# A graph network on one core: the gathers of z rows written out on GpSimd, with indices from the loaded table

## The chip, the cores and the metric

The kernel runs on one core of a Trainium2 chip. The metric is the time on the device in microseconds (us), the median of the runs. The engines are TensorE (PE in the profile; PEld its weight loads), VectorE (DVE), ScalarE (ACT), GpSimd (POOL) and SyncE (SP, which here only issues DMAs).

## The reference

A graph of 6250 nodes with 128 features and 200,000 edges, sorted by destination, goes through four graph layers. After each, the layer's result is added to x and normalized:

```python
x = layernorm(x + L0(x, W, attn_w, rel_emb, bias, src, dst, edge_type))   # attention over edges
x = layernorm(x + L1(x, ...))                                            # mean over neighbours
x = layernorm(x + L2(x, ..., edge_weight))                               # three weighted convolutions
x = layernorm(x + L3(x, ..., edge_attr))                                 # filtered messages

# L0
z = h @ W.T
e = leaky_relu((z @ w1)[src] + (z @ w2)[dst])
num = exp(e - segment_max(e, dst)[dst])
alpha = num / segment_sum(num, dst)[dst]
h_agg = segment_sum((rel_emb[etype] * alpha)[:, None] * z[src], dst)
```

## The kernel before

The edges are padded to 196 groups (NG) of 1024, each held as 128 partitions by 8 columns (TILES). The stages are blocks of code, and at the end of a block all engines meet at a barrier.

- A prelude loads inputs and computes z for all nodes. The rows of z, 132 words with the attention scores beside the features (ZW), are stored to HBM as z_table.
- A short block (lines 574 to 722) finds, for each window of 8 destination nodes, which tiles of 128 edges belong to it. GpSimd meanwhile runs gather_pairs(e, 0, 4), the first 8 groups of z rows.
- The main build block (lines 746 to 994) turns the edges into two dense matrices in HBM, c_dense (counts) and w_dense (edge weights), by source block and destination. VectorE makes one-hot tiles in a ring of eight slots (lines 836, 839, 850), with other work on the edge tables between them. TensorE multiplies them into four PSUM windows (line 920). ScalarE copies a finished window to a staging buffer (line 984, into parts of A and H by turns) and clears it (line 968). SyncE stores each full half block of 64 nodes (line 754). A loop at the end repairs windows that a tile overran. GpSimd runs gather_pairs(e, 4, 98), the other 188 groups, on its own.
- The attention layer reads those rows group by group (line 1055). It uses no tile of the build block besides z_edges in HBM and a few tables.
- Then come the dense layers (line 1405), during which GpSimd scatters edge records by an unrolled loop (line 1546), and the last layer, with an unrolled loop of gathers (line 1637).

gather_pairs copies rows of z for every edge of a group into the buffer z_got and stores them to z_edges in HBM. z_got has two slots, used by turns. One gather is one indirect DMA of 128 rows, each chosen by an index in its partition (line 527). Eight make a group, and the group is stored by one DMA (put_group, line 512). Per slot, s_zgot counts landed gathers and s_zput landed stores. The store of a group is issued after the fourth gather of the next one. The order on GpSimd is that of the code. The loop runs over pairs of groups; since its index is a register, the eight index columns of a group are first copied from src_i to z_idx (line 523), and the gathers wait for the copy (s_zidx). The increments of note["pool"] after a wait count for nobody.

Of the kernel before, what the change touches and what calls it, by code (L numbers as in the profile page):

```python
# [6 lines left out]
P = 128  # L7
# [7 lines left out]
TILES = 8  # L15
GE = TILES * P
NG = -(-N_EDGES // GE)
# [50 lines left out]
i32 = mybir.dt.int32  # L68
# [5 lines left out]
def build_program(nc, T, out):  # L74
    ctx = ExitStack()
    with ctx:
        def sb(name, shape, dt=f32, of=ctx):
            return of.enter_context(nc.sbuf_tensor(name, shape, dt))
# [3 lines left out]
        def sem(name):  # L82
            live.append(nc.alloc_semaphore(name=name))
            return live[-1]
# [10 lines left out]
        def dram(name, shape, dt=f32):  # L95
            return nc.dram_tensor(name, shape, dt, kind="Internal").ap()
# [20 lines left out]
        src_i = sb("src_i", [P, NG * TILES], i32)  # L117
# [34 lines left out]
        note = {n: nc.alloc_semaphore(name="note_" + n) for n in ("dve", "pe", "act", "pool", "sp")}  # L152
        Xv = X[:, :].rearrange("p (b f) -> p b f", f=F)
        z_table = dram("z_table", (NP_, ZW))
        z_edges = dram("z_edges", (NG, P, TILES, ZW))
# [344 lines left out]

        building = ctx.enter_context(ExitStack())
        z_got = sb("z_got", [P, 2, TILES, ZW], of=building)
        z_idx = sb("z_idx", [P, 2, TILES], i32, of=building)
        s_zidx = sem("bd_zidx")
        s_zgot, s_zput = ([sem(f"bd_{n}{s}") for s in range(2)] for n in ("zgot", "zput"))
        EARLY_PAIRS = 4

        def gather_pairs(e, lo, hi):
            def put_group(g, s, landed):
                e.wait_ge(s_zgot[s], landed)  # L510
                e.sem_inc(note["pool"], 1)
                e.dma_start(z_edges[bass.ds(g, 1), :, :, :].rearrange("a p t w -> (a p) t w"), z_got[:, s, :, :]
                            ).then_inc(s_zput[s], 16)

            last = e.alloc_register(f"bd_pool_last{lo}")
            e.reg_mov(last, max(2 * lo - 1, 0))
            with e.Fori(lo, hi) as i:
                for s in range(2):
                    g = i * 2 + s
                    with e.If(i > 0):  # L520
                        e.wait_ge(s_zput[s], i * 16)
                        e.sem_inc(note["pool"], 1)
                    e.tensor_copy(z_idx[:, s, :], src_i[:, bass.ds(g * TILES, TILES)]).then_inc(s_zidx, 1)
                    e.wait_ge(s_zidx, g + 1)
                    e.sem_inc(note["pool"], 1)
                    for t in range(TILES):
                        e.indirect_dma_start(  # L527
                            out=z_got[:, s, t, :], out_offset=None, in_=z_table,
                            in_offset=bass.IndirectOffsetOnAxis(ap=z_idx[:, s, t:t + 1], axis=0),
                        ).then_inc(s_zgot[s], 16)  # L530
                        if t == TILES // 2 - 1 and s:
                            put_group(i * 2, 0, (i + 1) * (16 * TILES))
                        elif t == TILES // 2 - 1:
                            with e.If(i > 0):
                                put_group(e.snap(last, min_val=0, max_val=NG - 1), 1, i * (16 * TILES))
                e.reg_mov(last, i * 2 + 1)
            if hi == NG // 2:
                put_group(NG - 1, 1, NG // 2 * 16 * TILES)
                for s in range(2):
                    e.wait_ge(s_zput[s], 16 * (NG // 2))  # L540

# [32 lines left out]
        with nc.Block() as block:  # L574
# [42 lines left out]
            @block.gpsimd  # L617
            def _(e):
                gather_pairs(e, 0, EARLY_PAIRS)
# [129 lines left out]
        with nc.Block() as block:  # L749
# [45 lines left out]
            @block.gpsimd  # L795
            def _(e):
                gather_pairs(e, EARLY_PAIRS, NG // 2)
# [1020 lines left out]
```

## Time and profile before

| | us |
|---|---|
| median of 3 runs | 10863.49 |
| the runs | 10908.15, 10863.49, 10833.27 |
| span of the profiled execution, first to last instruction | 10911.3 |
| GpSimd busy in it | 5544.8 (51%) |
| gathers of z rows, 1568 | 2098.9 |
| copies of index columns, 196 | 117.1 |
| TensorE's matmuls of the build, 14112 | 2519.8 |

The profiled execution is one of its own. It has no separate time beside its span, which lies 3 us above the slowest of the runs shown. In its timeline the short block with the first gathers runs from about 86 to 193 us and the main build block from there to about 3277 us. In the page's 40 slices one digit stands for 272.8 us, so these two blocks are the first twelve digits.

### The profile page before, as it was taken

How to read it: one execution, taken by the hardware profiler on the slowest of the kernel's cores; microseconds unless marked ns; L12 is line 12 of the kernel's file. 1: busy time of each engine (PE TensorE's matmuls, PEld its weight loads, DVE VectorE, ACT ScalarE, POOL GpSimd, SP SyncE). 2: the span in 40 equal slices, each digit the busy share in tenths (PEclk: the TensorE clock that was granted, in tenths of full speed). 3: DMA queues.
4: the chain of work that ended last, by engine and by line, in shares of the span. 5: the costliest groups of instructions: out<-in, count | busy, mean ns of one | idle time of the engine just before them, and what ended most of it. 6: DMA issues, size and time to landing. Idle time of an engine off the chain costs nothing. (4 is left out here: it accounts for less than half of the span.)

```text
span 10911.3 us, 154123 instructions
## 1 busy us (share of the span) xinstructions
PE 8137.0 (75%) x38400; PEld 4981.9 (46%) x38401; DVE 4162.8 (38%) x9898; ACT 3246.9 (30%) x5364; POOL 5544.8 (51%) x5296
## 2 busy tenths in 40 slices
PE   2988888888776666555688797887886777877776
PEld 1544444444435555555333343333334555555554
DVE  5887777643336666665400000000002222222223
ACT  3012345645556665555100000000002222222222
POOL 5888887777710000000355555555434655665664
PEclk7999999999995665666788898888987777877777
DMA  4234455656644333322566576666762222222222
GB/s 113 72 112 137 161 184 201 234 200 205 215 163 144 123 111 105 98 92 88 180 272 238 232 292 229 264 254 227 283 241 81 62 59 59 66 59 58 63 61 53
DMA packets 563180, 1661.60 MB, mean 152 GB/s; under 512 B 115313, under 2 KB 312029, under 8 KB 519494
## 3 DMA queue, kind: packets, MB, share of 16 engines
q1 hardware_dynamic: 324442, 1129.76, 28.3%
q0 software_dynamic: 206976, 473.99, 14.8%
q10 hardware_dynamic: 31536, 54.94, 1.4%
q8 instruction: 130, 2.13, 0.1%
q14 instruction: 96, 0.79, 0.0%
HBM read 1174.46 MB, written 483.82 MB: 152 GB/s over the span
## 5 line engine op out<-in xcount | busy, mean ns | idle before, releaser
L920 PE MATMUL wide<-ring 128*128 128x392 bf16 x14112 | 2519.8, 340 | 541.5 <-DVE ring L850 253.7
L527 POOL DMA_INDIRECT z_got<-z_table,z_idx x1568 | 2098.9, 1339 | 595.2 <-issue 468.7
L1546 POOL DMA_INDIRECT sorted_recs<-dn_rec_in,type_f x1568 | 1523.6, 972 | 1300.1 <-DMA dn_rec_in<-in_records 835.0
L1637 POOL DMA_INDIRECT l_rows<-h_table,l_recs x1568 | 1582.1, 1009 | 1176.0 <-DMA l_recs<-sorted_recs 725.3
L920 PEld LDWEIGHTS wide<-ring 128*128 128x128 bf16 x14112 | 1410.4, 100 | 1650.7 <-issue 900.1
L1405 PE MATMUL wide<-stream,X 128*128 128x512 f32 (+1 forms) x2548 | 1149.3, 602 | 255.2 <-issue 230.3
L1055 POOL DMA_DIRECT2D rows<-z_edges x196 | 103.5, 528 | 2055.9 <-PE wide L362 1849.1
L373 PE MATMUL wide<-rows,onehot 128*128 128x130 f32 x3904 | 858.1, 407 | 283.1 <-DVE A L390 283.1
L373 PE MATMUL wide<-l_rows,l_onehot 128*128 128x128 f32 x3904 | 669.5, 321 | 503.4 <-issue 326.7
L373 PEld LDWEIGHTS wide<-rows,onehot 128*128 128x128 f32 x3904 | 793.8, 310 | 341.4 <-DVE A L390 341.4
L1405 PEld LDWEIGHTS wide<-stream,X 128*128 128x128 f32 x2548 | 493.9, 201 | 876.7 <-issue 869.0
L373 PEld LDWEIGHTS wide<-l_rows,l_onehot 128*128 128x128 f32 x3904 | 596.4, 230 | 560.6 <-issue 358.6
L1532 DVE TENSOR_TENSOR A<-A,wide 128x512 f32<-128x512 f32 (+1 forms) x13 | 8.5, 657 | 2076.4 <-DMA range_src<-small 1751.3
L839 DVE TENSOR_TENSOR ring<-ring,parts 128x1536 bf16<-128x1536 bf16 (+1 forms) x394 | 692.5, 1758 | 65.9 <-issue 65.9
L1405 PE MATMUL wide<-stream,A 128*128 128x512 f32 (+1 forms) x1274 | 576.9, 603 | 126.9 <-issue 123.7
L1736 DVE TENSOR_TENSOR l_rows<-l_filters,l_rows 128x1024 f32<-128x1024 f32 x196 | 240.6, 1228 | 1107.3 <-ACT l_filters L1714 844.8
L968 ACT COPY wide<-zero_f 128x784 f32<-128x784 f32 x788 | 642.2, 815 | 66.1 <-PEq L574 17.1
L1405 PE MATMUL wide<-stream,H 128*128 128x512 f32 (+1 forms) x1274 | 574.9, 602 | 116.4 <-issue 110.3
L836 DVE TENSOR_TENSOR ring<-iota_h,src_r 128x512 bf16<-128x512 f16 (+1 forms) x394 | 271.6, 689 | 1015.6 <-PE wide L920 703.6
L984 ACT COPY A<-wide 128x784 f32<-128x784 f32 x392 | 318.0, 811 | 968.5 <-PE wide L920 844.9
L850 DVE TENSOR_SCALAR ring<-iota_h,slot_at 128x784 bf16<-128x784 f16 (+1 forms) x1568 | 596.6, 443 | 0.0
L1675 PE MATMUL wide<-w_L_gnn_W,l_hid 128*128 128x128 f32 x3136 | 498.6, 312 | 87.3 <-issue 85.8
(260 smaller groups left out, 8430.1 us busy)
## 6 DMA issues: line engine op xcount, KB each, us to landing
stream<-w_dense SPq DMA_DIRECT2D x252, 1792.0 KB
stream<-c_dense SPq DMA_DIRECT2D x84, 1792.0 KB
z_edges<-z_got POOLq DMA_DIRECT2D x196, 528.0 KB
rows<-z_edges POOLq DMA_DIRECT2D x196, 528.0 KB
dst_bc<-in_dst_row SPq DMA_DIRECT2D x196, 512.0 KB
c_dense<-A SPq DMA_DIRECT2D x49, 1568.0 KB
w_dense<-A SPq DMA_DIRECT2D x49, 1568.0 KB
c_dense<-H SPq DMA_DIRECT2D x49, 1568.0 KB
```

Source lines behind the costliest of these rows:

```text
L373: ins = e.matmul(sums_bank[:, 0:width], lhsT=onehot[:, t, :], rhs=group_rows[:, t, 0:width], start=(t == 0), stop=(t == TILES - 1))
L527: e.indirect_dma_start(out=z_got[:, s, t, :], out_offset=None, in_=z_table, in_offset=bass.IndirectOffsetOnAxis(ap=z_idx[:, s, t:t + 1], a ...
L836: e.tensor_tensor(to[:, :, 0, :], iota_h[:, 0:P].unsqueeze(1).to_broadcast([P, n, P]), src_r[:, bass.ds(t, n)].unsqueeze(2).to_broadcast([ ...
L839: e.tensor_tensor(to[:, :, 1:4, :], to[:, :, 0:1, :].to_broadcast([P, n, 3, P]), parts[:, bass.ds(t, n), :].unsqueeze(3).to_broadcast([P, ...
L850: e.tensor_scalar(ring[:, at:at + spans * WC], iota_h[:, 0:spans * WC], slot_at[:, bass.ds(t + k, 1)], None, ALU.is_equal).then_inc(s_made, 1)
L920: ins = e.matmul(banks[:, bass.ds(to[v], 1), int(m > 0), 0:WC].rearrange("p a x -> p (a x)"), lhsT=slots[:, k, m * P:(m + 1) * P], rhs=slo ...
L968: e.copy(pairs[k].rearrange("p (a x) -> p a x", a=2)[:, :, 0:WC], zero_f[:, 0:1].unsqueeze(2).to_broadcast([P, 2, WC])).then_inc(s_gone, 1)
L984: e.copy(staging[k][:, :, :, WN * n:WN * (n + 1)], window(n % 4))
L1405: ins = e.matmul(agg_bank[i % 2][:, 0:w], lhsT=stationary[p][:, b, :], rhs=stream[:, l % STREAMS, 0:w // HB, k, :], start=(b == 0), stop=( ...
L1546: e.indirect_dma_start(out=sorted_recs, out_offset=bass.IndirectOffsetOnAxis(ap=pos_i[:, g * TILES + t:g * TILES + t + 1], axis=0), in_=re ...
L1637: e.indirect_dma_start(out=rows[:, k, t, :], out_offset=None, in_=h_table, in_offset=bass.IndirectOffsetOnAxis(ap=recs[:, k, t, R_DST:R_DS ...
L1675: ins = e.matmul(filtered[:, t * P:(t + 1) * P], lhsT=hid[:, g % 2, t * P:(t + 1) * P], rhs=W["L3_gnn_W2"][:, :], start=False, stop=(t % 4 ...
```

## The change

gather_pairs is written out for all groups instead of looping over pairs. Each gather takes its index column straight from src_i at a fixed place, so z_idx, its copies and s_zidx are gone. The order of gathers and stores, the two slots and the waits for landed gathers and stores stay. The increments of note["pool"] are left out. Nothing else in the program is changed.

```diff
-        z_idx = sb("z_idx", [P, 2, TILES], i32, of=building)
-        s_zidx = sem("bd_zidx")
...
         def gather_pairs(e, lo, hi):
-            def put_group(g, s, landed):
-                e.wait_ge(s_zgot[s], landed)
-                e.sem_inc(note["pool"], 1)
-                e.dma_start(z_edges[bass.ds(g, 1), :, :, :].rearrange("a p t w -> (a p) t w"), z_got[:, s, :, :]
-                            ).then_inc(s_zput[s], 16)
...
-            with e.Fori(lo, hi) as i:
-                for s in range(2):
-                    g = i * 2 + s
-                    with e.If(i > 0):
-                        e.wait_ge(s_zput[s], i * 16)
-                        e.sem_inc(note["pool"], 1)
-                    e.tensor_copy(z_idx[:, s, :], src_i[:, bass.ds(g * TILES, TILES)]).then_inc(s_zidx, 1)
-                    e.wait_ge(s_zidx, g + 1)
-                    e.sem_inc(note["pool"], 1)
-                    for t in range(TILES):
-                        e.indirect_dma_start(
-                            out=z_got[:, s, t, :], out_offset=None, in_=z_table,
-                            in_offset=bass.IndirectOffsetOnAxis(ap=z_idx[:, s, t:t + 1], axis=0),
-                        ).then_inc(s_zgot[s], 16)
...
+            def put_group(g):
+                e.wait_ge(s_zgot[g % 2], (g // 2 + 1) * (16 * TILES))
+                e.dma_start(z_edges[g, :, :, :], z_got[:, g % 2, :, :]).then_inc(s_zput[g % 2], 16)
+
+            for g in range(2 * lo, 2 * hi):
+                if g >= 2:
+                    e.wait_ge(s_zput[g % 2], 16 * (g // 2))
+                for t in range(TILES):
+                    at = g * TILES + t
+                    e.indirect_dma_start(
+                        out=z_got[:, g % 2, t, :], out_offset=None, in_=z_table,
+                        in_offset=bass.IndirectOffsetOnAxis(ap=src_i[:, at:at + 1], axis=0),
+                    ).then_inc(s_zgot[g % 2], 16)
+                    if t == TILES // 2 - 1 and g:
+                        put_group(g - 1)
             if hi == NG // 2:
-                put_group(NG - 1, 1, NG // 2 * 16 * TILES)
+                put_group(NG - 1)
                 for s in range(2):
                     e.wait_ge(s_zput[s], 16 * (NG // 2))
```

On GpSimd, at the start of the main build block, the body of the loop before reads as follows for the first of its two groups (bd_zput0 is the landed stores of slot 0, bd_zidx the copy, bd_zgot1 the landed gathers of slot 1):

```order
L520 UNCONDITIONAL_BRANCH [waits bd_zput0]
L523 ISA
L523 COPY z_idx<-src_i 128x8
L524 REGISTER_ALU
L527 DMA z_got<-z_table,z_idx 128x132 [waits bd_zidx]
L527 DMA z_got<-z_table,z_idx 128x132 x3
L535 ISA
L512 ISA [waits bd_zgot1]
L512 DMA z_edges<-z_got 128x1056
```

In the changed kernel the same engine has this for a group and the first half of the next, at the same place:

```order
L516 DMA z_got<-z_table,src_i 128x132 [waits bd_zput0]
L516 DMA z_got<-z_table,src_i 128x132 x3
L509 DMA z_edges<-z_got 128x1056 [waits bd_zgot1]
L516 DMA z_got<-z_table,src_i 128x132 x4
L516 DMA z_got<-z_table,src_i 128x132 [waits bd_zput1]
```

The copy, its wait, the branches and the register instructions are gone, and the waits for landed stores and gathers stand on the DMAs themselves. No instruction of another engine changes its place.

## Rows read from the trace of the kernel before

**Rows 1.** The page: span; TensorE and GpSimd over 40 slices, busy tenths.

```profile
span 10911.3 us, 154123 instructions
...
PE   2988888888776666555688797887886777877776
...
POOL 5888887777710000000355555555434655665664
```

**Rows 2.** Timeline at the blocks' ends: start, length, instruction [idle before, releaser].

```profile
193.70 0.46 POOL L523 COPY z_idx<-src_i 128x8 int32 x1 [7.37 <-POOLq L574]
...
3079.85 0.58 POOL L512 DMA_DIRECT2D z_edges<-z_got  x1 [8.37 <-DMA z_got<-z_table,z_idx]
...
3241.33 0.37 SPq L754 DMA_DIRECT2D c_dense<-H  x1
...
3277.68 0.56 POOL L1055 DMA_DIRECT2D rows<-z_edges  x1 [197.26 <-PEq L1165]
```

**Rows 3.** Waits, 700 to 2100: total us, times, longest.

```profile
PE wide L920 <- DVE ring L850: 208.0, 48, 5.8
...
DVE ring L836 <- PE wide L920: 180.9, 85, 7.0
```

**Rows 4.** Windows: busy us (instructions) by engine, TensorE clock, DMA share, GB/s.

```profile
core 0: us, PE busy (x) PEld busy (x) DVE busy (x) ACT busy (x) POOL busy (x), PEclk, DMA share, GB/s
...
2200.00:3080.00 880.00, 702.35 (x3907) 387.63 (x3906) 344.19 (x492) 451.92 (x559) 645.64 (x642) 0.97 0.61 206
2900.00:3080.00 180.00, 136.91 (x760) 75.46 (x761) 67.16 (x96) 97.77 (x122) 125.88 (x129) 0.97 0.65 220
3080.00:3200.00 120.00, 97.47 (x561) 54.41 (x559) 46.35 (x67) 74.35 (x92) 0.42 (x1) 1.00 0.40 146
```

**Rows 5.** Groups of GpSimd's instructions, 194 to 3085.

```profile
L527 POOL DMA_INDIRECT z_got<-z_table,z_idx x1504 | 2032.4, 1351 | 571.6 <-issue 449.9 <-POOL z_idx L523 115.6 <-DMA z_got<-z_table,z_idx 3.4
L523 POOL COPY z_idx<-src_i 128x8 int32 x188 | 115.1, 612 | 45.4 <-DMA z_edges<-z_got 37.0 <-POOLq L574 7.4
```

**Rows 6.** Timeline of GpSimd across one copy.

```profile
3059.60 0.97 POOL L527 DMA_INDIRECT z_got<-z_table,z_idx  x1 [0.80 <-issue]
3060.88 0.94 POOL L527 DMA_INDIRECT z_got<-z_table,z_idx  x1 [0.30 <-issue]
```

**Rows 7.** Lines 523 and 527: duration ns min/median/max.

```profile
L523 POOL COPY z_idx<-src_i x196: 187/218/3392, 86.1 to 3058.6; 128x8 int32 x196
...
L527 POOL DMA_INDIRECT z_got<-z_table,z_idx x1568: 939/1028/3963, 87.6 to 3070.5; - x196
```

**Rows 8.** Groups of GpSimd's instructions, whole span: the two unrolled stages.

```profile
L1637 POOL DMA_INDIRECT l_rows<-h_table,l_recs x1568 | 1582.1, 1009 | 1176.0 <-DMA l_recs<-sorted_recs 725.3 <-issue 450.7
L1546 POOL DMA_INDIRECT sorted_recs<-dn_rec_in,type_f x1568 | 1523.6, 972 | 1300.1 <-DMA dn_rec_in<-in_records 835.0 <-issue 465.1
```

**Rows 9.** Waits of ScalarE, 2200 to 3080, then 3080 to 3242.

```profile
ACT H L984 <- remote: 30.1, 15, 4.4
ACT A L984 <- remote: 15.2, 7, 4.3
...
ACT H L984 <- PE wide L920: 34.4, 32, 2.6
ACT A L984 <- PE wide L920: 24.4, 25, 2.5
```

**Rows 10.** Timeline: two stores of staging buffer A, the first copy into it after.

```profile
2945.03 0.37 SPq L754 DMA_DIRECT2D c_dense<-A  x1
...
2970.50 0.81 ACT L984 COPY A<-wide 128x784 f32<-128x784 f32 x1 [4.27 <-remote]
...
3175.95 0.37 SPq L754 DMA_DIRECT2D c_dense<-A  x1
...
3197.88 0.81 ACT L984 COPY A<-wide 128x784 f32<-128x784 f32 x1 [1.37 <-PE wide L920]
```

**Rows 11.** Line 839: duration ns min/median/max.

```profile
L839 DVE TENSOR_TENSOR ring<-ring,parts x394: 558/1759/1851, 219.9 to 3259.5; 128x1536 bf16<-128x1536 bf16 x196, - x1
```

More of the change, by code:

```diff
@@ L508, in gather_pairs @@
         def gather_pairs(e, lo, hi):
-            def put_group(g, s, landed):
-                e.wait_ge(s_zgot[s], landed)
-                e.sem_inc(note["pool"], 1)
-                e.dma_start(z_edges[bass.ds(g, 1), :, :, :].rearrange("a p t w -> (a p) t w"), z_got[:, s, :, :]
-                            ).then_inc(s_zput[s], 16)
-            last = e.alloc_register(f"bd_pool_last{lo}")
-            e.reg_mov(last, max(2 * lo - 1, 0))
-            with e.Fori(lo, hi) as i:
-                for s in range(2):
-                    g = i * 2 + s
-                    with e.If(i > 0):
-                        e.wait_ge(s_zput[s], i * 16)
-                        e.sem_inc(note["pool"], 1)
-                    e.tensor_copy(z_idx[:, s, :], src_i[:, bass.ds(g * TILES, TILES)]).then_inc(s_zidx, 1)
-                    e.wait_ge(s_zidx, g + 1)
-                    e.sem_inc(note["pool"], 1)
-                    for t in range(TILES):
-                        e.indirect_dma_start(
-                            out=z_got[:, s, t, :], out_offset=None, in_=z_table,
-                            in_offset=bass.IndirectOffsetOnAxis(ap=z_idx[:, s, t:t + 1], axis=0),
-                        ).then_inc(s_zgot[s], 16)
[L531 to L536, printed above, removed]
```

## Prediction

> **What bounds the kernel now.** I read the 40 slices first, because one core runs stages with different limits [rows 1]. What the reader is to see: GpSimd (POOL) is busy at 0.7 to 0.8 through the first eleven or so slices, then nearly idle, and TensorE's digits (8 and 7) run on to the end of that stage. The edited code is all of GpSimd's work in this stretch, the build of the two dense matrices, and nothing else of the program uses it. So the question is not how much GpSimd saves, but whether anything waits for it.
>
> The timeline at the two ends of the main block answers most of that [rows 2]. The first eight groups are gathered in the block before, and GpSimd stands 7.37 us at the barrier between the two. In the main block GpSimd issues its last store at 3079.85. The other engines go on: the last store of a half block of the matrices is issued at 3241.33, and GpSimd's next instruction, in the stage that reads the gathered rows, starts at 3277.68 after 197.26 us of idle time that TensorE ended. GpSimd is early at the first barrier by 7 us and at the second by nearly 200 us. A faster GpSimd can't end either block sooner by itself.
>
> Who does end the block? From 700 to 2100 TensorE and VectorE wait for each other: TensorE waits 208.0 us for the last one-hot of a tile (line 850), VectorE 180.9 us for ring slots to come free [rows 3]. From 2200 on VectorE is busy 344 of 880 us only, and TensorE 702, at a mean granted clock of 0.97 [rows 4]; there the ring of four PSUM windows, which ScalarE empties and clears, and the stores of the half blocks set the pace. Neither pair takes anything from GpSimd. What GpSimd shares with them is the DMA engines, and the port through which VectorE holds it up, so the side effects need a price.
>
> **What the change removes on GpSimd.** Per group of eight gathers it removes the copy of eight index columns and the wait for that copy. In the whole main block the copies took 115.1 us for 188 [rows 5]. A gather that follows another starts 0.30 us after it, one that follows the copy 0.80 us [rows 6], so the wait costs 0.50 us more, or 188 x 0.50 = 94 us. Together 209 us. That is the upper end. The copy took 187 ns at least, 218 in the median and 3392 at most [rows 7]: the long ones were held up, and what held them up may hold the next gather instead. Then only 188 x 0.187 = 35 us and the 94 go, 129 us in all. The gathers themselves show the same holding (1028 ns in the median, 1351 in the mean) [rows 5, 7], instruction by instruction, so I count an instruction's delay as its own and take 200 us. GpSimd's last store then comes at about 3079.85 - 200 = 2880. The branches and register instructions of the loop go too; they lie in the gaps above and I give them no price of their own.
>
> **What it adds there.** Nothing is added but code: 1568 gathers and 196 stores written out, each in its old form and order, with the same waits for landed gathers and stores. Two costs can't be read from the loop. One is an index column taken from the wide table. The bounds are the unrolled scatter (972 ns in the mean, straight from such a table) and the unrolled gather of the last stage (1009 ns, from columns 66 words apart) against 1351 here [rows 5, 8]; both are lower, so I take none. The other is fetching straight-line code. Those two stages are written out in the same way, and the 1568 scatters of the first have 465.1 us of "issue" gaps, 0.30 each [rows 8], as in the loop. I take 0 and keep +0.2 us a gather as the bound, from the one gap in the loop that is wider (0.50). Up to 200 + 160 us over 1504 gathers, or 0.24 us each, it would still be hidden.
>
> The waits for a free slot of the gather buffer stay: the store of a group is issued after the fourth gather of the next, and four gathers pass before the slot is needed, before and after. In the early block the eight groups end some 8 x 1.1 = 9 us sooner; GpSimd waits 16 us instead of 7 at the same barrier. Cost 0.
>
> **What an earlier end is worth.** Here the trace has a comparison of its own [rows 4]. With gathers running, TensorE did 3907 matmuls in 880 us (4.44 per us), or 760 in the last 180 us (4.22 per us). After the last one it did 561 in 120 us (4.68 per us), at granted clock 1.00 against 0.97, with the DMA engines busy 0.40 instead of 0.61 to 0.65. ScalarE's waits say where part of it goes: up to 3080 it stood 45.3 us (30.1 + 15.2) before its window copies for a releaser outside the engines' records, and not once after it [rows 9]. One such wait: the store of staging buffer A is issued at 2945.03, and the first copy into A starts at 2970.50, 25.5 us later, after 4.27 us idle; with the gathers gone it is 3175.95 to 3197.88, 21.9 us, and the idle time is 1.37 [rows 10]. So the half-block stores land late while gathers share the DMA engines. If 200 us more run free of gathers, they take 200 x 4.44/4.68 = 190 us by the mean rate and 200 x 4.22/4.68 = 180 by the last one. A gain of 10 to 20 us; I take 14, since the clock's 0.03 need not follow the gathers.
>
> **What the denser gathers cost.** The same gathers now go out in 200 us less, about 7% closer together (200 of 2886). What they take from the others in the stretch from 2200 to 2880, by the rates above 5 to 10% of 680 us, is 34 to 68 us; 7% of it is 2 to 5 us. I take 3. VectorE I charge and credit with nothing: its longest regular instruction (line 839) lasts 1759 ns in the median and 1851 at most over the block [rows 11], while GpSimd's copies stretched to 3392; GpSimd waits for VectorE, not the other way.
>
> A rule of the Trainium skill speaks for more. "SBUF — State Buffer", section "SBUF: two separate sides", says that VectorE in some modes and GpSimd take one port pair as a lock, for a whole instruction, whichever starts first, so a copy on GpSimd may hold up VectorE as well. If each of 188 copies cost VectorE its own undisturbed 0.187 us, that is 35 us more. The row on line 839 shows at most 0.09 us in any one instruction, so the sum leaves it out.
>
> **The sum.** -14 + 3 = -11 us. The profiled execution has a span of 10911.3 us and would have 10900. It is slower than the median of the runs shown, 10863.49, and near the slowest, 10908.15; taken off the median it gives 10852.5. A measurement of this kernel can tell about 1% (109 us) from no change; this is a tenth of that.
>
> **The rivals.**
> First, the edit saves GpSimd nothing, since VectorE sets its pace: the removed copies' delay moves to the gathers. For: a gather lasts 1.35 us in the mean against 1.03 in the median, so much of GpSimd's time is being held. Against: the 0.50 us gaps are its own. Result 0, 10863.
>
> Second, slower: denser gathers delay the half-block stores. It acts from 2200 to 2880, where some 28 half blocks of 24.5 us are stored, and a store that lands late holds ScalarE's next copy and then TensorE. If the landing (25.5 us) grows by the full 7%, that is 1.8 us for each, 50 us, less the 14 gained at the end: +36, 10899. It turns the sign from 0.5 us (2%) per half block on. Against: only 45.3 us of such waits stand in 36 half blocks today, so most stores land in time. The Trainium skill, "DMA: Bandwidth & Descriptors", section "Queues, rings and completion order", has each DMA engine take turns between the queues packet by packet, which would be this rival's mechanism.
>
> Third, slower: a written-out gather costs more than in the loop. From 0.24 us each GpSimd ends the block; at 0.4 us it would end at 2880 + 1504 x 0.4 = 3482, some 240 us after the stores' 3241, so 11090. The unrolled stages speak against it.
>
> Fourth, faster: the copies did hold up VectorE. -11 - 35 = -46, 10817. By the lock rule of the SBUF page named above this would be the result; the row of line 839 doesn't support it. From 2200 on VectorE has slack, so only the two thirds of the copies before that could count, and 125 x 0.187 = 23 us is the likelier size.
>
> **Chances.** The forecast 0.64, the first rival 0.10, the second 0.12, the third 0.03, the fourth 0.11. All but the third stay inside 1%. The bounds of the costs reach from -46 to +36 around 10863, 10817 to 10899; the three runs spread from -30 to +45 about their median, but a median moves less. I give 10815 to 10895, which leaves out the third rival and the outermost of the rest. Faster by over 1% needs ten times the forecast: 0.02. Slower by over 1% is the third rival and a little of the unknown: 0.04. Same: 0.94.
>
> **What the profile after would show.** Right: no copy rows on GpSimd, every gather after a 0.30 us gap save where it waits for a DMA, the last store of the build near 2880 instead of 3079.85, the mean gather still near 1.35 us, and the next GpSimd instruction after it still near 3270, with some 390 us idle before. TensorE's rate should be near 4.68 matmuls per us from that end on, and unchanged before. The 7.37 us wait at the first barrier should be near 16. Wrong: gathers over 1.45 us or gaps over 0.5 us (third rival), ScalarE's waits of the unseen kind well over 45 us before the gathers' end (second), or VectorE's idle time between 700 and 2100 lower than now (fourth). What would upset all of it is a gather that GpSimd issues late enough to be the block's end.

## The result

The changed kernel took 11318.75 us in the median of four runs (11232.02 to 11378.49), the kernel before 10878.47 beside it (10833.27 to 10908.15). The ratio is 1.0392, with a 95% interval of 1.0355 to 1.0429. The forecast was 10852.5; the kernel is 440 us slower.

Both times belong to one of two surroundings that this study met. In later measurements the kernel before took either about 9560 us or 10,870 to 10,970, with under 1% between the executions of a measurement. It didn't go with the chip: one chip showed 9566 at one time and 10,970 at another. What makes the difference is not known. It has to be told here, because the result depends on it: where the kernel before takes 9560 us, the change costs nothing.

### The profile after

First the page of the changed kernel: span, and the busy tenths of TensorE, VectorE and GpSimd in 40 slices of 283 us.

```profile
span 11322.2 us, 152046 instructions
...
PE   3987778731888566665568889898787777777776
...
DVE  5877767610444566666540000000001222222223
...
POOL 5888888876000000000035555555553566666563
```

Against [rows 1] there is a hole: in the ninth and tenth slice TensorE is at 3 and 1 and VectorE at 1 and 0, while GpSimd works on at 7 and 6. The windows give it in numbers (columns as in [rows 4]).

```profile
2400.00:2800.00 400.00, 54.25 (x156) 20.61 (x156) 12.62 (x18) 15.71 (x20) 294.81 (x322) 0.52 0.36 105
2900.00:3600.00 700.00, 584.96 (x3314) 326.40 (x3313) 292.70 (x419) 393.97 (x485) 0.00 (x0) 0.98 0.39 142
```

From 2400 to 2800 TensorE does 156 matmuls in 400 us. The kernel before has this for the same stretch of time:

```profile
2400.00:2800.00 400.00, 323.60 (x1796) 178.80 (x1794) 155.36 (x222) 203.00 (x251) 294.51 (x292) 0.97 0.61 208
```

It does 1796. In the changed kernel GpSimd runs 322 instructions meanwhile, and the DMA engines are *less* busy than before (0.36 against 0.61). Once the gathers are over, TensorE does 3314 in 700 us, 4.73 per us.

The timeline of GpSimd at its first gather after the barrier and at its last instructions of the build, with the next block's first one:

```profile
192.48 1.16 POOL L516 DMA_INDIRECT z_got<-z_table,src_i  x1 [14.47 <-POOLq L559]
...
2811.93 0.94 POOL L516 DMA_INDIRECT z_got<-z_table,src_i  x1 [0.30 <-issue]
2813.18 0.94 POOL L516 DMA_INDIRECT z_got<-z_table,src_i  x1 [0.30 <-issue]
2817.72 0.58 POOL L509 DMA_DIRECT2D z_edges<-z_got  x1 [3.61 <-DMA z_got<-z_table,src_i]
...
3779.68 0.56 POOL L1040 DMA_DIRECT2D rows<-z_edges  x1 [961.38 <-PEq L1150]
```

These rows answer to [rows 2]: the last store comes 262 us earlier, and the next block begins 502 us later, after GpSimd stood 961 us. So GpSimd ended early as was forecast, and the others didn't keep their pace. The whole profiled execution is 411 us longer (11322.2 against 10911.3): behind this block it took 91 us less, nearly all of it in the dense layers, where the change does nothing and where other executions differ as much.

The waits of 194 to 3700 us in total, times, longest. The profile writes "remote" where the awaited count was raised, but no instruction that raises it had ended within the 1.5 us before; "issue" is a time in which it shows nothing waited for.

```profile
DVE ring L821 <- remote: 417.5, 12, 115.3
...
ACT H L969 <- remote: 264.5, 14, 58.5
DVE ring L821 <- issue: 230.7, 72, 129.4
ACT A L969 <- remote: 211.2, 12, 64.8
```

The kernel before has over the same stretch:

```profile
DVE ring L836 <- remote: 50.8, 7, 11.0
ACT H L984 <- remote: 30.8, 16, 4.4
ACT A L984 <- remote: 15.8, 8, 4.3
```

That is 97 us in all against 893. What such waits are is seen in the timeline of the hole.

```profile
2558.94 0.81 ACT L969 COPY H<-wide 128x784 f32<-128x784 f32 x1 [31.91 <-issue]
...
2559.81 0.82 ACT L953 COPY wide<-zero_f 128x784 f32<-128x784 f32 x1
...
2561.51 4.10 PE L905 MATMUL wide<-ring 128*128 128x392 bf16 x12 [29.46 <-issue]
...
2570.97 0.96 POOL L516 DMA_INDIRECT z_got<-z_table,src_i  x1 [0.33 <-issue]
...
2592.54 0.81 ACT L969 COPY H<-wide 128x784 f32<-128x784 f32 x1 [31.91 <-issue]
2592.66 0.73 DVE L821 TENSOR_TENSOR ring<-iota_h,src_r 128x512 bf16<-128x512 f16 x1 [129.37 <-issue]
```

ScalarE clears a window at 2560.6, and TensorE starts the tile that waited for it 0.9 us later: that direction is quick. TensorE ends the tile at 2565.6. The count of ended tiles (s_room) is what ScalarE waits for before the next copy and VectorE before the next ring slots. Both go on within 0.12 us of each other, at 2592.54 and 2592.66, 27 us after the tile's end. Two engines that wait for one semaphore and start together, with no work in between, are read here as a signal of TensorE that came late. (The profile calls these two waits "issue", since the trace lacks the raise of the count there, so the 893 us are less than all.) At 2367.65 and 2367.77 the same pair starts together after 11 and 27 us of "remote". The ring has eight slots and the windows are four, so one late signal soon stops all three.

The trace also holds the times at which the counts were raised, and they bear this reading out. Every "remote" wait of ScalarE and VectorE in the two profiles of this section (24 and 7 before, 26 and 12 after) ended with a raise of s_room; none ended with the landing of a store. The count should rise when TensorE ends a tile, and the trace shows how long after the tile's end it does:

| profiles | raises of s_room recorded, of 1570 | over 0.1 us late | over 1.5 us late | latest, us |
|---|---|---|---|---|
| the nine with the kernel before at 9560 | 1559 to 1569 | 0 | 0 | 0.015 |
| kernel before (10911 us) | 1388 | 186 | 27 | 3.3 |
| changed kernel (11322 us) | 1431 | 208 | 55 | 52.7 |

The counts that ScalarE (s_gone) and VectorE (s_made) raise are never over 0.1 us late in this block, in any of the twenty profiles. So the lateness in this block is TensorE's alone, and the kernel before has it already. It isn't TensorE that stands still: in the kernel before 101 raises are over 0.5 us late, and in 85 of these cases TensorE had begun further matmuls by then. And it ends with GpSimd's stream. Of the tiles that TensorE ends more than 10 us after GpSimd's last store in the build, 364 in the changed kernel and 61 before, none has a late raise, nor have the 1368 of the other late profiles; every one of these raises is recorded. Two limits remain: the ends of matmuls are modelled, and while the gathers run in the late profiles, up to a sixth of the raises of a count isn't recorded.

### The profile page after: what moved, and what is told of

It reads as the page before. It is cut to its first block and busy times, and to the rows that moved or that the text cites. A ratio compares the mean times of both kernels' runs of the same rounds, so it can differ in the third digit from the quotient of the medians.

```text
span 11322.2 us, 152046 instructions
## 1 busy us (share of the span) xinstructions
PE 8178.7 (72%) x38400; PEld 4994.2 (44%) x38401; DVE 4160.6 (37%) x9898; ACT 3248.0 (29%) x5364; POOL 5381.4 (48%) x5100
## 5 line engine op out<-in xcount | busy, mean ns | idle before, releaser
L905 PE MATMUL wide<-ring 128*128 128x392 bf16 x14112 | 2583.4, 345 | 981.3 <-issue 472.5
L516 POOL DMA_INDIRECT z_got<-z_table,src_i x1568 | 2076.5, 1324 | 617.9 <-issue 485.9
L373 PE MATMUL wide<-l_rows,l_onehot 128*128 128x128 f32 x3904 | 646.5, 316 | 524.2 <-issue 272.5
L969 ACT COPY H<-wide 128x784 f32<-128x784 f32 x392 | 318.0, 811 | 1080.3 <-PE wide L905 634.6
```

Source lines behind the costliest of these rows:

```text
L373: ins = e.matmul(sums_bank[:, 0:width], lhsT=onehot[:, t, :], rhs=group_rows[:, t, 0:width], start=(t == 0), stop=(t == TILES - 1))
L516: e.indirect_dma_start(out=z_got[:, g % 2, t, :], out_offset=None, in_=z_table, in_offset=bass.IndirectOffsetOnAxis(ap=src_i[:, at:at + 1] ...
L905: ins = e.matmul(banks[:, bass.ds(to[v], 1), int(m > 0), 0:WC].rearrange("p a x -> p (a x)"), lhsT=slots[:, k, m * P:(m + 1) * P], rhs=slo ...
L969: e.copy(staging[k][:, :, :, WN * n:WN * (n + 1)], window(n % 4))
```

## Experiments

Eighteen runs after the first. All are measured beside the kernel before on the same chip; "quick" below means that it took about 9560 us there, "late" about 10,880. The table's last four columns are from the profiled execution of each run, which is one of several and need not be a typical one. Most of all in s3: its profiled execution took 11,026 us, and the other three, from which its ratio comes, 11,201 to 11,322. The profiled one of s4 (11,232) is the slowest of its four. So a profile's columns go with its span, and not with the ratio.

| run | pause per group | kernel before, us | ratio, 95% interval | span, us | GpSimd's last store | late signals | next block |
|---|---|---|---|---|---|---|---|
| kernel before | copy, loop | late | 1 | 10911 | 3079.8 | 97 | 3277.68 |
| first result | none | 10878.47 | 1.0392 [1.0355, 1.0429] | 11322 | 2817.7 | 893 | 3779.68 |
| e1 | copy | 9566.28 | 1.0005 [0.9995, 1.0014] | 9561 | 2950.0 | 0 | 3206.15 |
| e2 | none, loop | same | 0.9999 [0.9989, 1.0008] | 9558 | 2922.4 | 0 | 3206.31 |
| e3 | idle copy | same | 1.0005 [0.9996, 1.0015] | 9569 | 2951.3 | 0 | 3209.22 |
| e4 | none, 3 copies | same | 1.0008 [0.9998, 1.0017] | 9578 | 3034.7 | 0 | 3216.24 |
| r1 | none | 9559.6 | 0.9997 [0.9988, 1.0006] | 9555 | 2905.3 | 0 | 3203.99 |
| r2 | none, loop | same | 0.9998 [0.9989, 1.0007] | 9557 | 2926.4 | 0 | 3210.06 |
| r3 | idle copy | same | 1.0003 [0.9994, 1.0012] | 9565 | 2958.4 | 0 | 3216.93 |
| r4 | none | 9548.4 | 0.9999 [0.9989, 1.0008] | 9549 | 2915.9 | 0 | 3203.58 |
| e5 | 2 idle copies | same | 1.0010 [1.0000, 1.0019] | 9557 | 3032.6 | 0 | 3217.95 |
| e6 | copy, loop, load | 10969.55 | 1.0010 [0.9989, 1.0031] | 10967 | 3282.6 | 157 | 3350.07 |
| e7 | none, load | same | 1.0256 [1.0168, 1.0345] | 11197 | 3033.5 | 469 | 3569.23 |
| r5 | idle copy | 10881.88 | 1.0088 [1.0046, 1.0130] | 10969 | 2906.5 | 271 | 3387.17 |
| r6 | none, loop | same | 1.0178 [1.0123, 1.0233] | 11154 | 2859.5 | 567 | 3543.11 |
| r7 | 2 idle copies | same | 1.0069 [1.0047, 1.0090] | 10975 | 3033.3 | 235 | 3334.11 |
| s1 | copy | 10865.85 | 1.0179 [1.0131, 1.0228] | 10995 | 2920.8 | 324 | 3374.80 |
| s2 | wait for landing | same | 1.0102 [1.0062, 1.0141] | 10937 | 3395.1 | 64 | 3409.68 |
| s3 | none, loop | same | 1.0374 [1.0310, 1.0438] | 11024 | 2866.1 | 389 | 3457.59 |
| s4 | none | same | 1.0208 [1.0132, 1.0284] | 11230 | 2834.1 | 706 | 3630.32 |

"Late signals" is the sum of the "remote" waits of VectorE's first one-hot and ScalarE's copies into H and A from 194 to 3700 us (893 is 417.5 + 264.5 + 211.2 above).

### e1: the copy back

```diff
+                e.tensor_copy(z_idx[:, g % 2, :], src_i[:, g * TILES:(g + 1) * TILES]).then_inc(s_zidx, 1)
+                e.wait_ge(s_zidx, g + 1)
...
-                        in_offset=bass.IndirectOffsetOnAxis(ap=src_i[:, at:at + 1], axis=0),
+                        in_offset=bass.IndirectOffsetOnAxis(ap=z_idx[:, g % 2, t:t + 1], axis=0),
```

> The written-out code with the copy of the index columns and its wait put back, the gathers reading the copy. Theory A (the pause of about 1 us per group, copy plus wait, is what let the other engines' signals through): about 10880, as before, no stretch in which TensorE falls under 200 matmuls per 100 us. Theory B (gathers that take their index from the wide table disturb the others): also about 10880. Theory C (straight-line code on GpSimd disturbs the others): about 11320, as the changed kernel.

### e2: the loop kept, only copy and wait taken out

Without the copy a loop can't reach the index columns of each group, so this kernel, here and as r2, r6 and s3, gathers the rows of groups 0 and 1 over and over. It reads other addresses than the rest, which is a second difference beside the missing pause.

```diff
-                    e.tensor_copy(z_idx[:, s, :], src_i[:, bass.ds(g * TILES, TILES)]).then_inc(s_zidx, 1)
-                    e.wait_ge(s_zidx, g + 1)
...
-                            in_offset=bass.IndirectOffsetOnAxis(ap=z_idx[:, s, t:t + 1], axis=0),
+                            in_offset=bass.IndirectOffsetOnAxis(ap=src_i[:, s * TILES + t:s * TILES + t + 1], axis=0),
```

> The loop of the kernel before without copy and wait; every group gathers by one of two fixed sets of eight index columns of the wide table, so the rows of z that are gathered are those of groups 0 and 1 throughout, and the attention layer's sums are not the reference's. Theory A: about 11300, the starved stretch appears in a loop too. Theory B: about 11300. Theory C: about 10860.

### e3: the changed kernel with the copy and its wait, which nobody reads

```diff
+                e.tensor_copy(z_idx[:, g % 2, :], src_i[:, g * TILES:(g + 1) * TILES]).then_inc(s_zidx, 1)
+                e.wait_ge(s_zidx, g + 1)
```

> The changed kernel with the copy and its wait put back per group although nobody reads the copy; the gathers still take their indices from the wide table. Theory A: about 10880. Theory B: about 11320. Theory C: about 11320.

### e4: three small copies per group, with no wait

```diff
+                for k in range(3):
+                    e.tensor_copy(z_pad[:, g * 3 + k, :], src_i[:, g * TILES:g * TILES + 1])
```

> The changed kernel with three small copies per group on GpSimd that nobody waits for or reads, each into a column of its own, some 0.6 us or more in all. If only the length of the pause counts (theory A as a matter of rate), about 10900 to 11000; if it takes a wait on a semaphore of its own, about 11300; theories B and C: about 11320.

All four came out at 1.000 to 1.001, and the kernel before at 9566 instead of 10,878. Whatever had cost 440 us wasn't there, so the four expectations were neither met nor refuted. What they do show is that the removed and added instructions cost nothing as instructions: 588 extra copies on GpSimd (e4) made 1.0008. If each copy took its undisturbed 0.187 us from VectorE, as in the prediction's fourth rival, e4 would have been up to 110 us or 1.0115, and 73 us or 1.008 if only the two thirds count that lie before VectorE has slack. The Trainium skill's lock rule for the port pair, quoted in the prediction ("SBUF — State Buffer", "SBUF: two separate sides"), has no measurable price for copies of this size here.

### r1 to r3: the changed kernel again, beside two of the others

> The changed kernel itself, unaltered, beside the kernel before on one chip. The four kernels of the first experiments ran within 0.1% of the kernel before at 9566 us, with or without the copy and in a loop or not. If the slowdown of 3.9% belongs to the change everywhere, the ratio is about 1.04. If it needs something that only the chip of the first comparison had (where the kernel before took 10878), the ratio is 0.998 to 1.002 wherever the kernel before takes about 9570.

> The loop without copy and wait, index columns of groups 0 and 1 throughout, again. If this call falls on surroundings like those of the first comparison (the kernel before over 10800), a ratio of about 1.04 says that the missing pause does the harm and not the straight-line code, and 1.00 the opposite. With the kernel before near 9570: 1.00.

> The changed kernel with an idle copy and its wait per group, again. With the kernel before over 10800: 1.00 if the pause of GpSimd protects the other engines, 1.04 if the table or the straight-line code does the harm. With the kernel before near 9570: 1.00.

The changed kernel itself is at 0.9997 when the kernel before takes 9560 us. So the first result wasn't a property of the code alone.

### r4 and e5: a third time, and two pauses per group

e5 is e3 with the copy and its wait before the first and the fifth gather of each group.

```diff
+                    if t % 4 == 0:
+                        n = 2 * g + t // 4
+                        e.tensor_copy(z_idx[:, n % 2, :], src_i[:, g * TILES:(g + 1) * TILES]).then_inc(s_zidx, 1)
+                        e.wait_ge(s_zidx, n + 1)
```

> The changed kernel unaltered, on whatever chip this call gets. Two comparisons stand against each other: 1.039 where the kernel before takes 10878, 0.9997 where it takes 9560. Where the kernel before comes near 9560 I expect 1.000 again; near 10870, 1.04.

> The changed kernel (written-out code, indices from the wide table) with a small copy that nobody reads and a wait for it before the first and the fifth gather of each group, so GpSimd pauses about 1 us every four gathers; in the kernel before it is every eight. With the kernel before near 9560: GpSimd's last store moves some 200 us back, to about 3150, still under the build's end near 3180, so 1.000 to 1.003. Where the kernel before takes 10870 and the changed one 1.04: theory A (pauses protect the other engines) says 1.00 or lower; theory B (the wide table) and theory C (straight-line code) say 1.04.

Both ratios are as expected here. GpSimd's last store moved less than I had given: to 3033 and not 3150.

### e6 and e7: are the DMA engines what gives way?

Both get 98 extra copies of 2.16 MB from HBM to HBM, issued on ScalarE's queue during the build: e6 the kernel before, e7 the changed one.

```diff
+                        e.dma_start(junk[bass.ds(i * 2 + k, 1), :, :, :].rearrange("a g p w -> (a g) p w"),
+                                    T["records"][0:JG, :, :]).then_inc(s_junk, 16)
```

> The kernel before with extra memory traffic in the build block: ScalarE issues one copy of 2.16 MB from HBM to HBM (eight groups of records into a scratch tensor) after each half block, 98 in all, on its own queue; the results are the same. By 212 MB read and as many written in some 3 ms the DMA engines should be near full late in the block, and the block longer, by perhaps 100 to 600 us over 9550. This is the baseline for the next run.

> The changed kernel with the same extra traffic. If crowded DMA engines or a crowded HBM were the missing condition of the first comparison, it starves here: at least 150 us (1.5%) slower than the loaded kernel before, with stretches of long waits in which GpSimd keeps its full pace. If the condition is another one (something of that chip's that slows the delivery of signals, with the DMA packets themselves no slower), the two loaded kernels agree within 0.3%.

These met the late surroundings. The window of e6, to be compared with that of the kernel before above:

```profile
2400.00:2800.00 400.00, 312.78 (x1723) 172.26 (x1724) 150.86 (x216) 195.45 (x242) 259.30 (x262) 0.96 0.77 272
```

The load moved GpSimd's last store 203 us back (3282.6), but didn't lengthen the kernel (1.0010, where I had given 100 to 600 us), though the DMA engines were at 0.77 and moved 272 GB/s, against 0.61 and 208 without it. So a busier set of DMA engines doesn't by itself make this cost. The loaded e7 lost 1.0256, between s4 (1.0208) and the first result (1.0392), both without a load; no unloaded run of the changed kernel stood beside it.

### r5 to r7: the pause, where the cost is there

> The changed kernel with the idle copy and its wait per group, once more. The last call fell on a chip where the kernel before takes 10970 and the loaded changed kernel 1.026 of it. If this call gets such a chip: theory A (GpSimd's pause protects the other engines) 1.00; theory B (the wide index table) and theory C (straight-line code) 1.03 to 1.04. With the kernel before near 9560: 1.000, nothing learned.

> The loop without copy and wait, rows of groups 0 and 1 gathered throughout. On a chip where the kernel before takes over 10800: theory A 1.03 to 1.04, since GpSimd issues eight gathers and a store without a pause in a loop as well; theory C (straight-line code) 1.00; theory B 1.03 to 1.04.

> The changed kernel with a copy and a wait every four gathers. On a chip where the kernel before takes over 10800: theory A says 1.00 or a little under, since GpSimd rests twice as often as in the kernel before; theories B and C 1.03 to 1.04.

The loop loses 1.8% when copy and wait go, where I had given 3 to 4% or nothing. Written out with an idle copy and wait it loses 0.9%, with two 0.7%, where theory A had no loss and the others 3 to 4%. Both of the latter read their indices from the loaded table, so the table alone doesn't bring a loss of 2 to 4%. A missing pause costs something, in a loop as well, but no theory gave these sizes, and the written-out kernel without a pause wasn't among these three.

### s1 to s4: the square of form and pause, and a pause without a copy

s2 adds only a wait, for the landing of the group before:

```diff
+                if g:
+                    e.wait_ge(s_zgot[(g - 1) % 2], ((g - 1) // 2 + 1) * (16 * TILES))
```

> The changed kernel, written out, with the copy and its wait put back and the gathers reading the copied columns, measured where the kernel before takes some 10,880 us. It differs from the kernel before only in being written out and in the increments that count for nobody. If the pause is all that matters: 0.998 to 1.003 of the kernel before. If the written-out form has a cost of its own, which the idle copy (1.0088) and two pauses (1.0069) left open: 1.006 to 1.012 again. Where the kernel before takes some 9,560 us, all theories expect 0.999 to 1.001.

> The changed kernel, and before the first gather of every group GpSimd also waits until the group before has landed. No copy and no other instruction is added, so this is a pause of a few us per group in which no gather is under way at all. If what protected the other engines was that the queue of gathers stops for a moment: 0.998 to 1.010 of the kernel before, as with the idle copies. If it was the copy as an instruction on GpSimd: 1.02 to 1.04, as in the changed kernel. GpSimd would end later than in the changed kernel, by 188 landings of 2 to 3 us, so near 3250 to 3400, which by itself may cost up to 100 us (1.01) where the kernel before takes 9,560 us.

> The loop of the kernel before without copy and wait, fixed index columns (it gathers the rows of groups 0 and 1 throughout, so its output differs). In the same surroundings as the changed kernel it tells how much of the cost is the missing pause and how much the written-out form. Pause alone: 1.03 to 1.045 as the changed kernel. Part of it the written-out form: 1.012 to 1.025, as in its first run there. Where the kernel before takes some 9,560 us: 0.999 to 1.001.

> The changed kernel beside the other three. Where the kernel before takes some 10,880 us: 1.03 to 1.045 if its first measurement (1.039) holds, against 1.026 seen once under a load of copies. Where it takes some 9,560 us: 0.999 to 1.001.

Again late surroundings. Here the loop without a pause lost more (1.0374) than the written-out form (1.0208), the other way round than r6 (1.0178) and the first result (1.0392). The size of the loss differs between measurements by two per cent of the kernel; that of the forms can't be told from it. All four without a pause and without a load lie between 1.018 and 1.039. s4, expected at 1.03 to 1.045, missed at 1.0208. s1, which is the kernel before but for being written out, is at 1.0179, where I had given 0.998 to 1.003 or 1.006 to 1.012: both missed. Its interval overlaps that of s4, so in this measurement a copy and its wait per group bought the written-out kernel nothing that the times can tell.

s2 is the telling one, by its profile more than by its time: 1.0102 [1.0062, 1.0141] is at the edge of what I had given for a protecting stop, and its interval touches that of s4. Windows of s2 (first) and of s4, columns as in [rows 4]:

```profile
2400.00:2800.00 400.00, 331.50 (x1876) 185.20 (x1877) 163.00 (x234) 212.07 (x262) 245.75 (x223) 0.98 0.58 199
```

```profile
2400.00:2800.00 400.00, 138.77 (x623) 68.17 (x622) 54.55 (x78) 66.04 (x82) 303.37 (x315) 0.68 0.43 135
```

With the wait TensorE does 1876 matmuls, against 623 without it and 1796 in the kernel before. The waits of s2, 194 to 3700:

```profile
POOL z_got L518 <- DMA z_got<-z_table,src_i: 640.7, 187, 6.4
...
DVE ring L823 <- remote: 34.9, 5, 8.5
...
ACT A L971 <- remote: 14.8, 5, 4.9
...
ACT H L971 <- remote: 13.8, 7, 3.5
```

GpSimd pauses 187 times for 3.4 us in the mean, and the late signals come to 64 us, fewer than the 97 of the kernel before. By the raises of s_room, 16 are over 1.5 us late, against 69 in s4 and 84 in s1. No copy is in it. So a stop of the gathers protects, without any copy as an instruction. Whether it takes the stop itself, or only fewer gathers per us (GpSimd ends 561 us later than in s4), no run separates. What s2 still loses is another thing, which its timeline shows:

```profile
3391.30 0.94 POOL L518 DMA_INDIRECT z_got<-z_table,src_i  x1 [0.30 <-issue]
3395.11 0.58 POOL L509 DMA_DIRECT2D z_edges<-z_got  x1 [2.87 <-DMA z_got<-z_table,src_i]
3409.68 0.56 POOL L1042 DMA_DIRECT2D rows<-z_edges  x1 [13.99 <-PEq L1152]
```

SyncE's last store of the matrices is at 3243.53, where the kernel before has 3241.74, but GpSimd ends at 3395 and now closes the block itself, 132 us later than before. That is more than the run's 111 us (1.0102). The cover over GpSimd's work is gone.

In the table the profiles of the late surroundings without a load, sorted by GpSimd's last store (2818, 2834, 2860, 2866, 2906, 2921, 3033, 3080, 3395), have late signals of 893, 706, 567, 389, 271, 324, 235, 97 and 64 us. But for one pair it is one order over both forms: the faster GpSimd gets through its gathers, the more signals come late. The spans go with it: 10,911 to 10,995 us for the five profiles with 64 to 324 us, then 11,024, 11,154, 11,230 and 11,322 for 389, 567, 706 and 893. Part of that runs the other way: while VectorE stands, nothing stretches the gathers (0.94 us in the timeline above, 1.35 in the mean), so GpSimd gets denser still. A stall feeds itself in this way, and that may be why one kernel loses 2.1% in one measurement and 3.9% in another.

## Why the prediction was wrong

**GpSimd isn't the bound: held.** Nearly every gather follows after 0.30 us, the wait at the first barrier was 14.5 us (16 forecast), and TensorE's rate after the gathers 4.73 per us (4.68). The last store was forecast at 2880 and came at 2818 and 2834 in late surroundings, 2905 and 2916 in quick ones. The price behind it was put in the wrong place: I gave the 200 us to the copy and its wait and nothing to the loop. s1 keeps both and, merely written out, ends 159 us before the kernel before; taking them out then gives 87 us (s4). In quick surroundings they are worth 45 us (2950 in e1, 2905 in r1).

**The step that failed** is "What GpSimd shares with them is the DMA engines, and the port", and with it the term for denser gathers, +3 us. There is a third thing that GpSimd's stream of gathers touches: the time at which TensorE's count of ended tiles rises and is seen by ScalarE and VectorE. Its measured size was +502 us at the end of the block in the first result (440 in the medians of the whole) and +353 in s4, and nothing that can be measured in quick surroundings. The scaling of that term (7% denser, so 7% more loss) assumed a smooth cost. The runs show a steep one: GpSimd's end moves by 8% (3080 to 2834) and the late signals from 97 to 706 us.

**The reading of [rows 9] was false.** I took the 45.3 us of ScalarE's "remote" waits for half-block stores that land late among the gathers. The times of the raises say that all of them ended with TensorE's count, and none with a landing. In r4 the stores share the DMA engines with the gathers at 0.65 of their time from 2400 to 2800, more than the 0.61 of the kernel before, and its waits from 194 to 3700 hold no "remote" row at all. Nor had I asked what the copies after the first of a half block wait for: only that one waits for a store. The rows that showed the danger were before me, with a story attached that made them harmless, and the third to warn was VectorE's, which can't wait for such a store (33.8 us from 2200 to 2880).

**The earlier end, -14 us: not there.** Taking its 45 us as a cost of sharing, I let a gather-free stretch repay it. In quick surroundings, where no signals are late, TensorE isn't faster without the gathers: in r4 it does 1917 matmuls from 2400 to 2800, 4.79 per us, and 1095 from 2920 to 3160, after the last one, 4.56 per us (a later part of the block, as in [rows 4]). The whole change is worth 0.9997 and 0.9999 there, -3 and +1 us, inside the intervals.

**The rivals.** The first (nothing changes, 10863) is what quick surroundings show, by its number and not by its mechanism, since GpSimd did end earlier there. The second named the right sign and the right place in the profile to look, waits of the unseen kind "well over 45"; they are 476 us for ScalarE alone. Its mechanism, landings of stores, isn't what the waits show (none ended with one), and its +36 us was a twelfth of the loss. The third (dear straight-line gathers) is refuted: they take 1.34 us in the mean, 1.35 before. The fourth is refuted by e4, at least for copies as small as those.

**The chance.** 0.04 for slower by over 1% was too little by a misuse of averages: I priced what GpSimd does to the others from the trace of one kernel, at one density, and nothing in it bounded another density.

**Still open.** Why TensorE's signals come late at all, and what separates quick from late surroundings. The kernel before has late signals too, above all outside the build (last section), but no run changed those stages, so what they cost it isn't shown. Also why a pause by a copy in the written-out form (1.007 to 1.018) protects less than in the loop: the loop's pause is longer, 115.6 us of idle time behind 188 copies [rows 5] against 34.5 in s1, which fits the order above, but no run gave the written-out form that length alone. And the loops without a pause gather other rows than the rest, which no run separates.

## What to carry to other kernels

An engine with 200 us of slack before a barrier isn't always free to go faster. A copy and a wait between bursts of indirect DMAs may be part of what keeps TensorE's signals near their time; before removing them, look for "remote" waits on engines that wait for nothing but another compute engine, and take them as a warning. Where such waits are found, a stop of the stream per group (here a wait for the landing) takes most of them away (64 us left of 706), at the price of GpSimd's own time, so it pays only while GpSimd still ends under cover. And measure the kernel before again beside every variant: a difference of 4% was there in one of the two surroundings and absent within 0.1% in the other.

## What the runs showed of the hardware

The same program took 9550 or 10,880 us, 14% apart. This is the page of r4, the changed kernel in quick surroundings: TensorE's and GpSimd's slices.

```profile
span 9548.5 us, 152046 instructions
...
PE   1998888888888566665555999999999888888886
...
POOL 4888888887771000000001667777774577777775
```

The hole isn't there. The builds of r4 and of the kernel before end at 3204 and 3278, 74 us apart; the rest of the program, in which the two are the same code, takes 6345 and 7634. TensorE's late 9s and 8s are 6s to 8s in [rows 1]. By stage, from the first to the last DMA or matmul named, with the recorded raises that come over 0.1 us after the TensorE instruction that makes them:

| stage | what GpSimd issues | kernel before, us | r4, us | TensorE's late raises before | in r4 |
|---|---|---|---|---|---|
| main build block | 1504 gathers | to 3278 | to 3204 | 186 of 1388 | 0 of 1563 |
| attention layer | loads of rows, none indirect | 1963 | 1964 | 0 of 677 | 0 of 677 |
| dense layers | 1568 scatters | 2908 | 2198 | 171 of 401 | 0 of 467 |
| last layer | 1568 gathers | 2582 | 2036 | 515 of 902 | 0 of 1026 |

So the late surroundings cost the attention layer nothing and the two unrolled stages 1256 us of the 1289. TensorE's signals are late in the three stages in which GpSimd issues indirect DMAs for milliseconds, and not in the one between them; in the dense and the last layer 522 of them are over 1.5 us late. ScalarE's are late in none, VectorE's in the dense layers alone (9 of 50). This goes together; that the late signals make the 1256 us isn't shown. TensorE's granted clock goes with it as well: 0.87 from 5300 to 7000 in the kernel before and 0.99 in r4, but 0.63 in both in the attention layer; which comes first no run tells.

The DMA queues weren't slower: packets of GpSimd's queue took 16.4% of 9548.5 us of the 16 engines, 1566 us, in r4, and 14.8% of 10911.3, 1615, in the kernel before.

A signal of TensorE can reach its waiters tens of us late (27 us in the timeline above, waits of up to 129 us) while the busy engine, GpSimd, waits in this block for nothing but its own DMAs. The Trainium skill, "VectorE: DVE Perf Modes", in its section on TRN2's errata, warns that a high rate of on-completion semaphore increments from one engine can deadlock another, and that kernels with dense increments from multiple engines should space them. No run here deadlocked, and none shows that this is the same mechanism; what the runs do agree with is the advice, since spacing GpSimd's stream, whose DMAs raise a semaphore each, took the late signals from 706 us (s4) to 64 (s2).
